# Two merges of a divide-and-conquer eigensolver rewritten as one block, and two convolutions changed from full fp32 to three float32r passes

## The reference

```python
# layer 0: spectral convolution; U are the eigenvectors of the normalised Laplacian
_, U = jnp.linalg.eigh(L_norm)                      # 64 x 64
agg = einsum('mn,bnd->bmd', U.T, features)
out = relu(agg @ W1 + b1) @ W2 + b2
x = layernorm(x + einsum('nm,bmd->bnd', U, out))
# layer 1: two graph convolutions (256 -> 256 each), then four LSTMs over windows of nodes
h = relu(einsum('ts,bsh->bth', adj, x @ Wg0 + bg0))
h = relu(einsum('ts,bsh->bth', adj, h @ Wg1 + bg1))
```

## Time and profile before

| | us |
|---|---|
| median of 3 runs (2260.89 to 2263.25) | 2262.45 |
| profiled execution, its own time | 2259.93 |
| span of the profiled execution | 2257.9 |
| from the end of the sweeps to the first `spread` (both merges) | 98.6 |
| from the first `spread` to the end of `spectral_and_mixing` | 244.5 |

### The profile page before, as it was taken

How to read it: one execution, slowest core, us unless ns; L and a number is a source line. 1 busy time by engine, 2 the same in 40 slices (tenths; PEclk the granted TensorE clock), 3 DMA queues, 4 the chain that set the end, 5 groups by cost and what they waited for, 6 DMA issues and landing times. The chain is left out here.

```text
span 2257.9 us, 31660 instructions
## 1 busy us (share of the span) xinstructions
PE 1814.0 (80%) x9300; PEld 1509.0 (67%) x9300; DVE 1458.4 (65%) x5905; ACT 865.9 (38%) x1772; POOL 649.7 (29%) x1034
## 2 busy tenths in 40 slices
PE   3454333201999989999999999999999798989997
PEld 2333333201777778888889999988888686866674
DVE  7998999886555456545544444434443676867886
ACT  2332222200333356433333333323332465746664
POOL 0010444301222257533333323432222111631111
PEclk9999666655999999999999999999999899989999
DMA  6000000000100100000000000000000411310111
GB/s 182 1 2 1 1 1 1 2 0 0 47 38 38 47 14 19 14 9 9 8 11 10 0 9 9 1 1 0 0 19 0 196 61 53 101 50 29 38 38 47
DMA packets 44682, 62.59 MB, mean 28 GB/s; under 512 B 13968, under 2 KB 33296, under 8 KB 44432
## 3 DMA queue, kind: packets, MB, share of 16 engines
q1 hardware_dynamic: 43968, 61.05, 8.0%
q10 hardware_dynamic: 592, 0.17, 0.1%
HBM read 36.04 MB, written 25.17 MB: 27 GB/s over the span
## 5 line engine op out<-in xcount | busy, mean ns | idle before, releaser
L1886 ACT ACTIVATE l_gates<-ps,biases 128x512 f32<-128x512 f32 (+1 forms) x504 | 289.3, 636 | 502.9 <-remote 488.2
L1820 PE MATMUL ps<-l_nodes_in,l_even 128*128 128x512 f32 x1392 | 319.2, 389 | 0.5 <-remote 0.4
L1820 PE MATMUL ps<-l_nodes_in,kept 128*128 128x336 f32 (+1 forms) x1280 | 299.6, 351 | 8.9 <-remote 7.1
L1820 PEld LDWEIGHTS ps<-l_nodes_in,l_even 128*128 128x128 f32 x1392 | 261.0, 188 | 55.4 <-issue 1.3
L1931 DVE TENSOR_TENSOR l_gates<-l_gates 128x512 f32<-128x512 f32 (+1 forms) x72 | 49.8, 692 | 341.8 <-ACT l_gates L1886 341.8
L1775 POOL CAST l_nodes_in<-big 128x512 fp32r (+3 forms) x142 | 101.7, 745 | 546.6 <-remote 530.3
L1820 PEld LDWEIGHTS ps<-l_nodes_in,kept 128*128 128x128 f32 x1280 | 230.3, 189 | 35.2 <-issue 11.8
L1820 PE MATMUL ps<-l_state,l_even 128*128 128x512 f32 x960 | 220.8, 389 | 0.0
L1820 PEld LDWEIGHTS ps<-l_state,l_even 128*128 128x128 f32 x960 | 180.2, 188 | 37.4
L1778 POOL TENSOR_TENSOR l_nodes_in<-big,l_nodes_in 128x512 fp32r<-128x512 f32 (+1 forms) x142 | 201.0, 1436 | 5.7
L992 PE MATMUL ps<-w,sw_xT 128*128 128x128 f32 x256 | 59.0, 424 | 136.5 <-ACT sw_xT L856 136.5
(11 more groups left out here) (537 smaller groups left out, 3888.8 us busy)
## 6 DMA issues: line engine op xcount, KB each, us to landing
x<-in_x SPq DMA_DIRECT2D x4, 2048.0 KB, 16.9
residual<-s_x SPq DMA_DIRECT2D x16, 512.0 KB, 2.6
x_late<-residual SPq DMA_DIRECT2D x16, 512.0 KB, 10.4
normed<-j_x SPq DMA_DIRECT2D x16, 512.0 KB, 2.6
x_late<-normed SPq DMA_DIRECT2D x16, 512.0 KB, 3.3
out<-a_y SPq DMA_DIRECT2D x16, 512.0 KB, 2.9
l_raw<-in_L_gnn_W SPq DMA_DIRECT2D x16, 256.0 KB, 2.7
l_raw<-in_L_gnn_W SPq DMA_DIRECT2D x4, 512.0 KB, 3.6
```

The lines of the kernel that those rows point to most:

```text
L1820: return pe.matmul(ps[:, 4 * j + gate, 0:n], w[w_part][:, at:at + 128].bitcast(F32R), src[:, part, k, 0:n].bitcast(F32R), start=start, sto ...
L1886: act.activation(gates[:, j, gate, 0:n], ps[:, 4 * j + gate, 0:n], ACT.Tanh if gate == G else ACT.Sigmoid, bias=bias[:, gate * KD + j:gate ...
```

## The change

`merge` goes. A class `Merge` holds the tensors of one level, and `join_leaves` runs both merges, what was ahead of them and what was behind them in one block. The first merge works on 32 columns, the second on 64. The iteration runs on u = 1/root: a step is 7 instructions (one of them, the reciprocal of b, waits for b alone), unrolled, without a clear of the semaphore and without the clamps. `interval` (38 instructions, with `poles` 44) ends with a first step of its own, so that `seek` has 8 more. Its test compares the steps that give u[6] and u[7], against 2^-9, and its product on TensorE runs beside the last step. Vectors are turned and multiplied before they are normalised, the factor is put on afterwards, and ScalarE takes the copy of the turned vectors. GpSimd splits the two convolution weights in high and low parts in the same block (`aside`). In `spectral_and_mixing` both convolutions become three float32r passes (high by high, high by low, low by high): 24 matmuls of 256 columns and 12 of 512 per group. ACT's two moves write the high parts; two new DVE instructions `low` write the low parts, and `bias2` moves to the next step, ahead of them. Three intermediate tensors go: the ReLUs of ScalarE work in place, and DVE's writers wait for the reader on TensorE instead of for ACT.

The removed lines of `merge` are those printed above; in its place the diff shows the core of what is new.

```diff
-FIRST_NEWTON = 10
+FIRST_NEWTON = 9
...
+        "fold": np.arange(NODES)[:, None] % (2 * LEAF) == np.arange(2 * LEAF)[None, :],
+        "pair": np.arange(NODES)[:, None] // LEAF % 2 == np.arange(2 * LEAF)[None, :] // LEAF,
...
-def merge(nc, ctx, t, ps, leaf, lam, zbig, level):
...
+def join_leaves(nc, ctx, t, ps, leaf, lam, qT, m, aside):
...
+            def poles(g, lam):
+                s, chain, done = g.s, g.chain, g.done
+                dve.wait_ge(g.d_ready, 1)
+                dve.tensor_copy(g.d[:, :], g.D).then_inc(chain, done.one())
...
+            def interval(g, lam, rho, rho2):
...
+                ts(g.t1[:, :], g.rel[:, :], s["inv"], -1.0, ALU.mult, ALU.add).then_inc(chain, done.one())
...
+                stt(g.u[0], s["c"], s["rb"], s["first"], ALU.mult, ALU.add).then_inc(chain, done.one())
...
+            def newton(g, u, u_next, chain, done):
+                s = g.s
+                ts(g.t1[:, :], g.rel[:, :], u, -1.0, ALU.mult, ALU.add).then_inc(chain, done.one())
+                dve.wait_ge(chain, done.n)
+                dve.reciprocal(g.p[:, :], g.t1[:, :]).then_inc(chain, done.one())
+                dve.wait_ge(chain, done.n)
+                ttr(g.zp[:, :], g.p[:, :], g.zz[:, :], 1.0, 0.0, ALU.mult, ALU.add, s["a"]).then_inc(chain, done.one())
+                dve.wait_ge(chain, done.n)
+                ttr(g.junk[:, :], g.zp[:, :], g.p[:, :], 1.0, 0.0, ALU.mult, ALU.add, s["b"]).then_inc(chain, done.one())
+                b_at = done.n
+                ts(s["c"], u, s["a"], 1.0, ALU.mult, ALU.add).then_inc(chain, done.one())
+                dve.wait_ge(chain, b_at)
+                dve.reciprocal(s["rb"], s["b"]).then_inc(chain, done.one())
+                dve.wait_ge(chain, done.n)
+                stt(u_next, s["c"], s["rb"], u, ALU.mult, ALU.add).then_inc(chain, done.one())
+                dve.wait_ge(chain, done.n)
+            def seek(g):
+                s, chain, done = g.s, g.chain, g.done
+                for i in range(FIRST_NEWTON - 1):
+                    newton(g, g.u[i], g.u[i + 1], chain, done)
+                    if i == FIRST_NEWTON - 3:
+                        ts(s["now"], g.u[i + 1], s["side"], s["actc"], ALU.mult, ALU.mult).then_inc(chain, done.one())
+                        ts(s["was"], g.u[i], s["side"], 1 + 2.0 ** -9, ALU.mult, ALU.mult).then_inc(chain, done.one())
+                        dve.wait_ge(chain, done.n)
+                        tt(g.moving[:, :], s["now"], s["was"], ALU.is_gt).then_inc(g.moving_ready, 1)
+                u = g.u[FIRST_NEWTON - 1]
+                dve.wait_ge(g.total_ready, 1)
+                dve.tensor_copy(g.flag[:, :], g.total).then_inc(chain, done.one())
+                dve.wait_ge(chain, done.n)
+                with dve.If(dve.value_load(g.flag[0:1, 0:1]) != 0):
+                    with dve.Fori(0, MORE_NEWTON):
+                        dve.sem_clear(g.loop)
+                        newton(g, u, u, g.loop, Count())
+                return u
...
+            def vectors(g, u):
+                s, chain, done = g.s, g.chain, g.done
+                ts(g.t1[:, :], g.rel[:, :], u, -1.0, ALU.mult, ALU.add).then_inc(chain, done.one())
+                dve.wait_ge(chain, done.n)
+                dve.reciprocal(g.p[:, :], g.t1[:, :]).then_inc(chain, done.one())
+                dve.wait_ge(chain, done.n)
+                tt(g.vec[:, :], g.zs[:, :], g.p[:, :], ALU.mult).then_inc(g.vec_ready, 1)
+                dve.wait_ge(g.vec_ready, 1)
+                ttr(g.junk[:, :], g.vec[:, :], g.vec[:, :], 1.0, 0.0, ALU.mult, ALU.add,
+                    s["n2"]).then_inc(chain, done.one())
+                dve.wait_ge(chain, done.n)
+                tt(s["n2b"], s["n2"], s["nact"], ALU.add).then_inc(g.n2_ready, 1)
...
+            poles(M0, lam)
+            interval(M0, lam, rho[:, 0:1], rho2[:, 0:1])
+            dve.wait_ge(ct_ready, 1)
+            tt(coupleT[:, :], CT, t["half"][:, :], ALU.mult).then_inc(M1.chain, M1.done.one())
+            root = seek(M0)
+            vectors(M0, root)
+            eigenvalues(M0, root, lam, lam1[:, :])
+            norms(M0)
+            dve.wait_ge(M0.prod_ready, 1)
+            dve.wait_ge(M1.chain, M1.done.n)
+            ttr(junk[:, :], M0.PROD, coupleT[:, :], 1.0, 0.0, ALU.mult, ALU.add,
+                zcol[:, :]).then_inc(M0.chain, M0.done.one())
+            dve.wait_ge(M0.chain, M0.done.n)
+            ts(zrow[:, :], zcol[:, :], s0["y"], s0["w"], ALU.mult, ALU.mult).then_inc(zrow_ready, 1)
+            ts(znT[:, :], M0.PROD, s0["y"], s0["w"], ALU.mult, ALU.mult).then_inc(znt_ready, 1)
+            poles(M1, lam1[:, :])
+            interval(M1, lam1[:, :], rho[:, 1:2], rho2[:, 1:2])
+            dve.wait_ge(z1_ready, 1)
+            tt(z1[:, :], Z1, t["half"][:, :], ALU.mult).then_inc(z1_moved, 1)
+            root = seek(M1)
+            vectors(M1, root)
+            norms(M1)
+            dve.wait_ge(M1.prod_ready, 1)
+            dve.wait_ge(M1.chain, M1.done.n)
+            ts(ut[:, :, :], M1.PROD[:, None, :].to_broadcast([N, 2, N]), s1["y"], s1["w"], ALU.mult,
+               ALU.mult).then_inc(ut_moved, 1)
+            dve.wait_ge(u_ready, 1)
+            for rows in halves:
+                dve.tensor_copy(m["spread"][rows, rows], U[rows, :]).then_inc(u_moved, 1)
+            dve.tensor_reduce(m["rowsum"][:, :], U, AX_X, ALU.add).then_inc(u_moved, 1)
+            dve.wait_ge(u_moved, 3)
...
+            def turn_vectors(g):
+                pe.wait_ge(g.nact_ready, 1)
+                pe.matmul(g.VT, g.own[:, :], g.keep[:, :], start=True, stop=False)
+                pe.wait_ge(g.vec_ready, 1)
+                pe.matmul(g.VT, g.vec[:, :], ident, start=False, stop=True).then_inc(g.vt_ready, 1)
...
             def convolve1(g):
                 pe.wait_ge(a1_moved, g + 1)
                 if g:
-                    pe.wait_ge(b_moved, g)
-                for i in range(TILES):
-                    for k in range(KD):
-                        mm = pe.matmul(G[:, i, :], agg1[:, k, i * TILE:(i + 1) * TILE], w["wg0"][:, k, :],
-                                       start=k == 0, stop=k == KD - 1)
+                    pe.wait_ge(b_low, g)
+                for part, w_parts in ((HIGH, PARTS), (LOW, (HIGH,))):
+                    if part == LOW:
+                        pe.wait_ge(a1_low, g + 1)
+                    for i in range(TILES):
+                        for k in range(KD):
+                            for w_part in w_parts:
+                                mm = pe.matmul(G[:, i, :], agg1[:, part, k, i * TILE:(i + 1) * TILE].bitcast(F32R),
+                                               w["wg0"][:, w_part, k, :].bitcast(F32R),
+                                               start=part == w_part == HIGH and k == 0 and i % 2 == 0,
+                                               stop=part == LOW and k == KD - 1 and i % 2 == 1)
...
             def convolve2(g):
                 pe.wait_ge(b_moved, g + 1)
                 if g + 1 < GROUPS:
-                    pe.wait_ge(a1_moved, g + 2)
+                    pe.wait_ge(a1_low, g + 2)
                 else:
                     pe.wait_ge(c_summed, KD * g)
+                pe.wait_ge(b_low, g + 1)
                 for j in range(KD):
                     for k in range(KD):
-                        mm = pe.matmul(C[:, j, :], w["wg1"][:, k, j * 128:(j + 1) * 128], agg2[:, k, :],
-                                       start=k == 0, stop=k == KD - 1)
+                        for w_part, part in ((HIGH, HIGH), (LOW, HIGH), (HIGH, LOW)):
+                            mm = pe.matmul(C[:, j, :], w["wg1"][:, w_part, k, j * 128:(j + 1) * 128].bitcast(F32R),
+                                           agg2[:, part, k, :].bitcast(F32R), start=k == 0 and part == w_part,
+                                           stop=k == KD - 1 and part == LOW)
...
             def bias1(g):
                 dve.wait_ge(g_ready, g + 1)
                 if g:
-                    dve.wait_ge(h1_ready, g)
-                dve.tensor_tensor(g1sum[:, :, :], G, m["rowbias"][:, None, :].to_broadcast([128, TILES, WIDTH]),
+                    dve.wait_ge(b_ready, g)
+                dve.tensor_tensor(h1[:, :, :], G, m["rowbias"][:, None, :].to_broadcast([128, TILES, WIDTH]),
                                   ALU.add).then_inc(g_summed, 1)
...
+            def low(g, moved, agg, psum, given):
+                dve.wait_ge(moved, g + 1)
+                dve.tensor_tensor(agg[:, LOW].bitcast(F32R), psum, agg[:, HIGH], ALU.subtract).then_inc(given, 1)
             for s in range(STEPS):
                 if s < GROUPS:
                     bias0(s)
+                if s >= 3:
+                    bias2(s - 3)
+                if 2 <= s < GROUPS + 2:
+                    low(s - 2, b_moved, agg2, B, b_low)
+                if 1 <= s < GROUPS + 1:
+                    low(s - 1, a1_moved, agg1, A1, a1_low)
+                if s < GROUPS:
                     norm(s)
```

(53 more changed lines are left out.)

461 lines of the change are left out of this document (227 added, 234 removed).

## The result

The changed kernel is slower by 1.2%: 2290.68 us (median of 4 runs, 2290.55 to 2291.12) against 2262.41 (4 runs), ratio 1.0121, 95% interval 1.0109 to 1.0134. The forecast was 2212, and what happened is the mechanism of rival 3 in both merges (chance 0.02, 2289 us).

What follows compares the result with a forecast made beforehand. Bound by a chain of small DVE instructions in the merges and TensorE's queue in `spectral_and_mixing`, stages not overlapping. Merges save 37 us and convolutions 13.5: 2262.45 - 50.5 = 2212 us, range 2204 to 2226.

Steps and rivals of the forecast that it cites:

- rival 3: Merges: the branch of twenty more steps is taken; 2253 us if in the second merge, 2289 in both; chance 0.02.
- Does the branch stay untaken?: Merges' convergence test: at the tested eighth step roots change by at most 2^-47 and 2^-31, against 2^-9, so no branch.
- one step in hand: Merges' convergence test: claimed margin of one step; at the seventh step the largest changes are 2^-22.9 and 2^-7.5.
- The iteration: Merges' root steps: 1.70 us on 32 columns, 1.96 on 64, eight each; 29.3 for 56.4, 27.1 us saved.
- Setups: Ahead of each merge's steps: 47 DVE records at 0.176 us; 16.3 for 19.3, 3.0 us saved.
- Head, middle, end: Merges before, between and after the iterations: 0.2, 4.5 and 3.4 us saved.
- The split: GpSimd's splitting of convolution weights beside DVE in the merges' head: costs 1.3 us, bounds 0 and 4.5.
- The convolutions: `spectral_and_mixing`: float32r matmuls take 0.12 us at 256 columns; `convolve1` saves 0.55 us and `convolve2` 0.63 per group.
- rivals 1, 4 and 5: Convolutions: 256 columns stay at 0.153 us (2220, chance 0.12); loads not hidden (2249, 0.01); fp32 cost (2325, 0.03).
- The period: `spectral_and_mixing`, per group: 12.9 us for 13.94, set by a loop through DVE's `low`, longer than PE's 12.76.
- rival 2: `spectral_and_mixing`: the DVE loop is a microsecond longer, the period 13.9, nothing saved there; 2225 us, chance 0.06.
- The stage: `spectral_and_mixing`: thirteen shorter periods save 13.5 us, fill and drain nothing; bounds 5.2 to 14.2.

Runs made afterwards that it cites:

- the masked kernel: Changed kernel with the test for moving roots multiplied by the mask of active columns (`actc`) again: 2209.16 us, ratio 0.9763.
- the flag less 1 and less 4: Changed kernel with the flag read as the count less 1 in the first merge and less 4 in the second: 2206.96 us, one run.
- wider threshold: Changed kernel with the test's threshold widened from 1 + 2^-9 to a factor of 9: 2288.7 us, one run.

## Why the prediction was wrong, point by point

**The step that failed** is the paragraph "Does the branch stay untaken?". It asked whether the *roots* of the graph's matrix converge in time, and on that it was right: the count holds no active column, as the masked kernel and the flag less 1 and less 4 show. (Its "one step in hand" is only the step that runs behind the tested one: by its own numbers the second merge's 2^-7.5 one step earlier would not have passed 2^-9.) It never asked what a deflated column, which has no root to find, puts into the same count: 1 in the first merge and 4 in the second, and a single one is enough. The diff had the answer in two lines: `now` carries `actc`, `was` does not, and the multiplication of the verdict by `actc` (line 1163 of before) is gone. Rival 3 was given 0.02 for a margin that had nothing to do with it. Its price was right by two errors that cancel: 2212 + 77 = 2289 for 2209.2 + 81.5 = 2290.7, the base 3 too high and the branches 4.5 too low (the loop's own cost in a step is 0.4 where I had 0.1). All chances together, with the 0.01 that was left, make 1.01, a hundredth too much.

**The iteration**, 27.1 foreseen, 29.5 measured: the eight steps of the second merge and the test are 15.06 (524.19 to 539.25), those of the first 12.81; less 0.5 for each test 26.9 for my 29.3. A step takes 1.54 and 1.81 where I had 1.70 and 1.96. Most of the 0.15 is one link: c need not wait for the second reduction and starts 0.15 after it (538.54 to 538.69 in the second merge), where I had paid the full 0.26. Half a reciprocal did save 0.20 (0.345 for 0.545).

**Setups**, 3.0 foreseen, 5.4 measured: 6.56 and 7.33 for 7.7 and 8.3, 50 records at 0.131 and 0.147 in place of 0.176 each. The mean of the old setup priced the new one too high; this is near the bound that I gave for fewer stalls (0.15 each).

**Head, middle, end.** Without the split 0.7 saved for 0.2 (2.01 for 2.68); the middle, with test and flag, 4.7 for 4.5; the end 7.3 for 7.8. **The split** took 2.7 for my 1.3, inside the bounds. In sum 41.0 for 37 (98.64 - 57.64 in the masked kernel).

**The convolutions.** 256 columns cost 3.06/24 = 0.1275 us for my 0.12; the loads stayed hidden (24 matmuls with a load of 128 columns each, 0.1275 us each), so the measurement decides against the rule of the Trainium skill that the prediction set beside this term, and rivals 1, 4 and 5 are out. **The period** is 12.74, not 12.9: the DVE loop that I had as the setter ends in time. `relu1` ends 0.25 before `aggregate2` begins at 710.48, and DVE idles ahead of each `low` for ACT's move (timelines of ACT and of DVE, kernel after):

```profile
709.17 1.06 ACT L1716 ACTIVATE s_h<-s_h 128x1024 f32<-128x1024 f32 x1 [4.73 <-DVE s_h L1768]
...
721.90 1.06 ACT L1716 ACTIVATE s_h<-s_h 128x1024 f32<-128x1024 f32 x1 [4.73 <-DVE s_h L1768]
```

```profile
713.52 1.22 DVE L1782 TENSOR_TENSOR s_agg<-ps,s_agg 128x1024 fp32r<-128x1024 f32 x1 [0.70 <-ACT s_agg L1722]
716.26 1.23 DVE L1782 TENSOR_TENSOR s_agg<-ps,s_agg 128x1024 fp32r<-128x1024 f32 x1 [1.52 <-ACT s_agg L1712]
717.40 1.21 DVE L1537 TENSOR_TENSOR s_lnr<-ps,x 128x1024 f32<-128x1024 f32 x1
```

So the loop can do with some 12.73 - 0.25 = 12.5: from `norm`'s add to `relu1` it is 721.90 - 717.40 = 4.50 for my 4.72, taken from the earlier trace rows in a group where PE still waited, and its other parts are some 0.1 shorter each (`relu1` to the move 5.8 without the 0.25, `low` to `norm` 1.14). TensorE's queue alone sets the period, at the 12.76 that I had for it, and rival 2 is out too.

**The stage** gained 12.6 in this kernel for 13.5 forecast, and that is luck in part: the periods gave more, the two ends took some of it back. Its parts, in us, by TensorE's timelines: the fill from the first `spread` to the fourth, the thirteen groups from there to the last `aggregate2` but one, and the drain up to the LSTM's first product.

| kernel | fill | thirteen groups | drain | stage |
|---|---|---|---|---|
| before | 42.72 | 181.22 | 25.69 | 249.63 |
| after | 43.56 | 166.20 | 27.29 | 237.05 |
| after, test masked | 42.78 | 166.20 | 27.14 | 236.12 |
| after, wider threshold | 42.34 | 166.18 | 25.69 | 234.21 |
| old merges, new stage | 42.51 | 166.57 | 25.71 | 234.79 |

The thirteen groups save 15.0 (13 x 1.2 = 15.6, less 0.7 in the last of them). I had put fill and drain at nothing. For the drain that holds where it is short (25.69 in both stages: a shorter group, a longer wait for `low`), but with the new stage the fill varies from run to run by 1.2 and the drain by 1.6. The merges in front don't decide it: the kernel with the wider threshold has the new merges with both branches and the shortest stage. What differs is the granted clock, as the last section shows.

## What to carry to other kernels

When a change rewrites the test of a rarely taken branch, work out what *every* lane puts into the count, the masked and padded ones first, and only then whether the real ones converge; a verdict is masked last, after the comparison, since a mask on one side of it can make a false verdict, as here. Price the branch beside the gain: here it cost 82 us where the whole change was worth some 54. Off-path work on GpSimd is not free where DVE is the path; put it where DVE has slack.

## What the runs showed of the hardware

**GpSimd beside DVE.** GpSimd's four instructions (two casts of 0.61 us, two subtractions of 1.27) ended at about 451.56, 452.12, 453.47 and 454.70. Four DVE instructions on 64 x 64 lay beside them: line 1077 took 0.66 for 0.28, line 1080 0.49 for 0.19, line 1266 1.24 for 0.25, line 1077 again 1.33 for 0.27. They ended at 451.64, 452.16, 453.53 and 454.78, each within 0.1 us behind one of GpSimd's, as if each had been held until GpSimd's had ended and not merely slowed. The Trainium skill's "SBUF — State Buffer", section "SBUF: two separate sides", lets a GpSimd instruction and a DVE instruction exclude each other for the whole instruction where DVE has two SBUF inputs or runs in a two-port performance mode. Line 1077 has two tensor inputs and fits the first case; lines 1080 and 1266 have one, and whether they ran in such a mode no trace shows.

**The clock at the ends of the stage.** The granted clock in fill and drain differs from run to run of nearly the same stage. Windows of 10 us, the third and fourth from the first `spread`, first of the kernel after, then of the old merges with the new stage:

```profile
609.66:619.66 10.00, 7.63 (x49) 6.59 (x47) 6.22 (x16) 2.34 (x3) 1.23 (x2) 0.94 0.00 0
619.66:629.66 10.00, 9.98 (x66) 9.77 (x67) 4.98 (x8) 3.28 (x4) 2.36 (x1) 0.83 0.14 54
```

```profile
571.76:581.76 10.00, 8.04 (x49) 7.00 (x47) 5.83 (x14) 1.97 (x3) 1.23 (x2) 0.90 0.00 0
581.76:591.76 10.00, 9.57 (x73) 9.24 (x74) 6.43 (x12) 3.65 (x5) 2.35 (x1) 1.00 0.14 55
```

In the fourth window the one was granted 0.83 of full speed in the mean (part of it at 2.4, part at 1.2 GHz) and got through 66 matmuls, the other 1.00 and 73; seven matmuls are about 1 us. The drain shows it in one product, the last `convolve2` (timelines of PE, kernel before, after, and with the wider threshold):

```profile
787.40 3.70 PE L1558 MATMUL ps<-s_agg,wg 128*128 128x512 f32 x8 [1.11 <-ACT s_agg L1608]
```

```profile
814.70 4.57 PE L1675 MATMUL ps<-s_agg,wg 128*128 128x512 f32 x12 [2.46 <-DVE s_agg L1782]
```

```profile
813.82 2.96 PE L1675 MATMUL ps<-s_agg,wg 128*128 128x512 f32 x12 [2.46 <-DVE s_agg L1782]
```

The same twelve matmuls behind the same wait took 4.57 us at a mean granted clock of 0.63 and 2.96 at 1.00: 1.6 us, all of the difference between the two drains. The new stage waits longer there than the old one (2.46 us for 1.11, since `low` now lies between the move and the product), and in the fill too (2.39 ahead of the first `aggregate2` for 1.55). The old stage had 1.00 behind both waits. Whether the longer wait is what lets the clock fall in some runs and not in others was not tried.
